# One TanH for four gates, one operation for the transform's spread, two f16 parts: an LSTM attention step on one core

## What is computed

```python
def step(carry, tgt):                     # tgt: one row of layernorm(x), 512 wide
    s, c, alpha = carry                   # 64, 64, 64 per batch row
    f = conv(alpha, conv_w)               # width 101
    e = einsum('a,bta->bt', va, tanh(enc_proj + (s @ Wa_s.T)[:, None, :] + f @ Wa_f + ba))
    alpha_new = softmax(where(mask, e, -1e30))
    g = einsum('bt,btd->bd', alpha_new, hbatch)
    y = tanh(g @ L_gy_w.T + L_gy_b + s @ L_sy.T) @ L_yy_w.T + L_yy_b
    rec = tgt @ L_ys.T + s @ L_ss.T + g @ L_gs_w.T + L_gs_b
    ig, fg, cg, og = split(rec, 4)        # 64 each
    c_next = sig(fg) * c + sig(ig) * tanh(cg)
    s_next = sig(og) * tanh(c_next)       # sig(z) = tanh(z / 2) / 2 + 1 / 2
```

## Time and profile before

| | us |
|---|---|
| median of three runs | 1523.16 |
| the three runs | 1520.36, 1523.16, 1537.06 |
| the profiled execution | 1518.94 |
| its span, first to last instruction | 1516.8 |

### The profile page before, as it was taken

The page is one execution under the profiler, slowest core; times in us unless marked ns, Lnnn a source line. Parts: engine busy times, 40 slices in busy tenths (PEclk is TensorE's granted clock), DMA queues, the critical chain, the costliest instruction groups (busy, mean ns, idle before and its releaser), DMA issues.

```text
span 1516.8 us, 43579 instructions
## 1 busy us (share of the span) xinstructions
PE 1395.5 (92%) x17408; PEld 919.4 (61%) x17408; DVE 943.9 (62%) x4478; ACT 544.3 (36%) x2143; POOL 275.1 (18%) x743
## 2 busy tenths in 40 slices
PE   4743887899999999999999999999999999999988
PEld 2533666466665676666666765556666666666546
DVE  4898455366665666675666657766655566566643
ACT  1343132134333344333334434443433333333321
POOL 3334222211111111111011111231110011111111
PEclk8565797999999999999999999999998999999989
DMA  8623000000000000000000001210000000000000
GB/s 278 240 90 90 0 1 4 1 2 2 3 2 2 2 2 2 3 2 2 2 2 2 2 19 45 58 37 2 2 16 2 2 2 9 9 2 3 9 9 14
DMA packets 19551, 37.06 MB, mean 24 GB/s; under 512 B 8436, under 2 KB 11683, under 8 KB 19348
## 3 DMA queue, kind: packets, MB, share of 16 engines
q1 hardware_dynamic: 19348, 34.28, 6.9%
HBM read 32.18 MB, written 2.10 MB: 23 GB/s over the span
## 4 chain that ended last, share of the span: by engine, by line
PE 83%; DVE 9%; issue 3%; ACT 2%; SPq 1%; POOL 1%; DMA 0%; DVEq 0%; ACTq 0%; POOLq 0%
PE bank L1921 9%; PE bank L1842 9%; PE bank L1635 9%; PE bank L1864 8%; PE bank L1652 6%; PE bank L1896 6%; PE bank L1673 4%; PE bank L1870 4%; PE bank L1618 3%; PE bank L1878 3%; PE bank L1905 3%; PE bank L1884 2%; PE bank L1612 2%; PE bank L1566 2%; PE bank L1518 2%
## 5 line engine op out<-in xcount | busy, mean ns | idle before, releaser
L1842 PE MATMUL bank<-ctx_lgs,identb 128*128 128x512 f16 (+2 forms) x685 | 190.9, 356 | 0.0
L1921 PE MATMUL bank<-ker_mem,uh 128*128 128x128 f32 x1020 | 184.3, 304 | 0.7 <-DVE ker_mem L1121 0.4
L1921 PEld LDWEIGHTS bank<-ker_mem,uh 128*128 128x128 f32 x1020 | 137.0, 194 | 66.1 <-DVE ker_mem L1121 48.9
L1635 PE MATMUL bank<-xT,wbig 128*128 128x256 f16 x1008 | 162.9, 275 | 0.0
L693 POOL TENSOR_TENSOR sscale<-ex,rinv 128x8 f32<-128x8 f32 x256 | 51.0, 199 | 506.8 <-DVE rinv L1106 506.8
L1439 ACT ACTIVATE xs<-gat 64x8 f32<-64x8 f32 x255 | 52.9, 207 | 244.2 <-DVE gat L1117 244.2
L1425 ACT ACTIVATE ker_mem<-bank 128x128 f16<-128x128 f32 x256 | 71.0, 278 | 184.8 <-PE bank L1864 184.8
L1430 ACT ACTIVATE eh<-bank,nmx 128x8 f16<-128x8 f32 x256 | 68.5, 268 | 172.4 <-PE bank L1887 172.4
L689 POOL COPY sscale<-s 64x4 f32<-64x4 f32 x256 | 59.0, 230 | 388.6 <-DVE s L1136 388.6
L1652 PE MATMUL bank<-wbig,interT 128*128 128x512 f16 x378 | 125.6, 399 | 0.0
L1121 DVE TENSOR_TENSOR ker_mem<-inv,ahn 128x128 f32<-128x128 f32 x510 | 124.0, 285 | 0.1
(11 more groups left out here) (238 smaller groups left out, 3290.9 us busy)
## 6 DMA issues: line engine op xcount, KB each, us to landing
wbig<-d_gate_qT SPq DMA_DIRECT2D x4, 896.0 KB, 9.9
wbig<-d_up_qT SPq DMA_DIRECT2D x4, 896.0 KB, 20.7
wbig<-d_down_qT SPq DMA_DIRECT2D x1, 3584.0 KB, 31.5
x_sb<-d_x SPq DMA_DIRECT2D x16, 128.0 KB, 6.0
d_out<-x_sb SPq DMA_DIRECT2D x16, 128.0 KB, 2.3
sscale<-d_gate_sT SPq DMA_DIRECT2D x2, 896.0 KB, 8.3
sscale<-d_up_sT SPq DMA_DIRECT2D x2, 896.0 KB, 4.3
work<-d_g1T SPq DMA_DIRECT2D x8, 224.0 KB, 2.5
```

What stands on the lines that cost most here:

```text
L1635: last = mm(tile_bank(n)[:, lo:lo + QC], w[wi][:, kt, it * P:(it + 1) * P], x_part[q % 2][xi][:, kt, :], start=(kt == 0 and wi + xi == 0), ...
L1842: mm(bank[7][:, 0:n], identb[:], hg2[:, 0].rearrange("p h g -> p (h g)")[:, 0:n], start=True, stop=True)
L1921: mm(bank[0][:, 0:P], uh[:, h, :], qv[:, h, :, :], start=False, stop=False, skip_group_check=True)
```

## The change

**Gate rows.** The permutation of the gate rows on the host is gone: `gat` holds input (partitions 0 to 63) and forget (64 to 127) in columns 0 to 3, cell and output in columns 4 to 7. ScalarE takes one TanH of 128x8 into `tg`. VectorE now needs two products of 64x4 (one of them reads partitions 0 to 63 and writes 64 to 127), since the cell state lies in a tile of its own, `cell`, on partitions 64 to 127. The scalings of weights and biases move with the rows.

**Spread.** The two operations of L1121 become one of 128x256 with one semaphore, `q_ready`. TensorE waits for it ahead of both f32 products. The wait on `kept` moves behind `sh`, ahead of the f32 state `s2`, which is what the copy reads.

**Parts.** `lss3` and `enc3` (three bf16 parts) become `lss2` and `enc2` (two f16 parts), the identity becomes f16 (`identh`). L1870 shrinks from ten matmuls to six, L1618 from three to two.

**Fill.** Half a unit moves from the place ahead of L1887 to the one ahead of L1878.

```diff
-                def spread(h):
-
-                    return nc.vector.tensor_tensor(qv[:, h, :, :], inv[:].unsqueeze(1).broadcast_to([P, B, TH]),
-                                                   ahn[:, 4 * h:4 * h + 4].unsqueeze(2).broadcast_to([P, B, TH]), ALU.mult)
-
                 dve.wait_ge(s["ahn_ready"], l + 1)
-                spread(0).then_inc(s["q0_ready"], 1)
+                nc.vector.tensor_tensor(qv.rearrange("p i b t -> p (i b) t"), inv[:].unsqueeze(1).broadcast_to([P, 2 * B, TH]),
+                                        ahn[:].unsqueeze(2).broadcast_to([P, 2 * B, TH]), ALU.mult).then_inc(s["q_ready"], 1)
+
+                dve.wait_ge(s["tg_ready"], l + 1)
+                nc.vector.scalar_tensor_tensor(ab[J:P, 0:4], tg[0:J, par, 0:4], 1.0, tg[0:J, par, 4:8], ALU.add, ALU.mult)
+                nc.vector.scalar_tensor_tensor(ab[J:P, 4:8], tg[J:P, par, 0:4], 1.0, cell[J:P, par, :], ALU.add, ALU.mult).then_inc(s["ab_ready"], 1)
+                dve.wait_ge(s["ab_ready"], l + 1)
+                nc.vector.scalar_tensor_tensor(cell[J:P, 1 - par, :], ab[J:P, 4:8], 0.5, ab[J:P, 0:4], ALU.mult, ALU.add).then_inc(s["c_ready"], 1)
+
+                dve.wait_ge(s["tc_ready"], l + 1)
+                nc.vector.scalar_tensor_tensor(sh[:], tg[J:P, par, 4:8], 1.0, tc_sb[J:P, :], ALU.add, ALU.mult).then_inc(s["sh_ready"], 1)
                 dve.wait_ge(s["kept"], l + 1)
-                spread(1).then_inc(s["q1_ready"], 1)
-
-                dve.wait_ge(s["tg_ready"], l + 1)
-                nc.vector.scalar_tensor_tensor(ab[:], tfi[:], 1.0, xs[:, par, 0:8], ALU.add, ALU.mult).then_inc(s["ab_ready"], 1)
-                dve.wait_ge(s["ab_ready"], l + 1)
-                nc.vector.scalar_tensor_tensor(xs[:, 1 - par, 0:4], ab[:, 0:4], 0.5, ab[:, 4:8], ALU.mult, ALU.add).then_inc(s["c_ready"], 1)
-
-                dve.wait_ge(s["tc_ready"], l + 1)
-                nc.vector.scalar_tensor_tensor(sh[:], xs[:, par, 8:12], 1.0, tc_sb[:], ALU.add, ALU.mult).then_inc(s["sh_ready"], 1)
-                nc.vector.scalar_tensor_tensor(s2[:, 1 - par, :], xs[:, par, 8:12], 1.0, tc_sb[:], ALU.add, ALU.mult).then_inc(s["s_ready"], 1)
+                nc.vector.scalar_tensor_tensor(s2[:, 1 - par, :], tg[J:P, par, 4:8], 1.0, tc_sb[J:P, :], ALU.add, ALU.mult).then_inc(s["s_ready"], 1)
@@
                 act.wait_ge(s["g_ready"], l + 1)
-                nc.scalar.activation(xs[:, par, 4:12], gat[J:P, :], ACT.Tanh, scale=0.5)
-                nc.scalar.activation(tfi[:], gat[0:J, :], ACT.Tanh, scale=0.5).then_inc(s["tg_ready"], 1)
+                nc.scalar.activation(tg[:, par, :], gat[:], ACT.Tanh, scale=0.5).then_inc(s["tg_ready"], 1)
                 act.wait_ge(s["c_ready"], l + 1)
-                nc.scalar.activation(tc_sb[:], xs[:, 1 - par, 0:4], ACT.Tanh, scale=0.5).then_inc(s["tc_ready"], 1)
+                nc.scalar.activation(tc_sb[J:P, :], cell[J:P, 1 - par, :], ACT.Tanh, scale=0.5).then_inc(s["tc_ready"], 1)
@@
-                for j in range(3):
-                    mm(bank[0][:, 0:P], identb[:], enc3[:, j, :], start=(j == 0), stop=False, skip_group_check=True)
+                for j in range(2):
+                    mm(bank[0][:, 0:P], identh[:], enc2[:, j, :], start=(j == 0), stop=False, skip_group_check=True)
@@
                 for gp in range(2):
-                    for j, st in ((0, sh), (1, sh), (2, sh), (0, sl), (1, sl)):
-                        last = mm(bank[2][:, 4 * gp:4 * gp + 4], lss3[:, j, gp * P:(gp + 1) * P], st[:],
-                                  start=(gp == 0 and j == 0 and st is sh), stop=(j == 1 and st is sl), skip_group_check=True)
+                    for j, st in ((0, sh), (1, sh), (0, sl)):
+                        last = mm(bank[2][:, 4 * gp:4 * gp + 4], lss2[:, j, gp * P:(gp + 1) * P], st[:],
+                                  start=(gp == 0 and j == 0 and st is sh), stop=(st is sl), skip_group_check=True)
                 last.then_inc(s["sp_done"], 1)
 
-                fill(UNIT, main_first, 384)
+                fill(UNIT + HALF_UNIT, main_first, 384)
                 pe.wait_ge(s["th_s"], l + 1)
@@
-                fill(UNIT, main_first)
+                fill(HALF_UNIT, main_first)
                 pe.wait_ge(s["th_lo_ready"], l + 1)
@@
                 fill(2 * UNIT, side_first)
+                pe.wait_ge(s["q_ready"], l + 1)
                 for h in range(2):
-                    pe.wait_ge(s[f"q{h}_ready"], l + 1)
                     mm(bank[0][:, 0:P], uh[:, h, :], qv[:, h, :, :], start=False, stop=False, skip_group_check=True)
                 fill(UNIT + HALF_UNIT, side_first)
@@
             dve.wait_ge(s["scale_ready"], 1)
-            in_parts(lss3[:], lssT[:])
+            in_halves(lss2[:], lssT[:])
@@
             dve.wait_ge(s["setup_cp"], 1)
-            in_parts(enc3[:], enc[:])
+            in_halves(enc2[:], enc[:])
```

More of the change, by code:

```diff
@@ L76, in shape_constants @@
         "c_time2": np.stack([np.tile(np.arange(TH), B), np.tile(np.arange(TH, T), B)]).astype(f32),
-        "c_gatescale": np.stack([np.where(np.arange(P) < J, 1.0, 2.0), np.ones(P)], 1).astype(f32),
+        "c_gatescale": np.stack([np.ones(P), np.where(np.arange(P) < J, 2.0, 1.0)], 1).astype(f32),
         "c_batchsel": (bm[None] == four).astype(f32),
@@ L137, in build @@
         enc = sb("enc", [P, P])
[L138 removed]
+        enc2 = sb("enc2", [P, 2, P], F16)
         hg = sb("hg", [P, 2, 256])
@@ L166, in build @@
         sl = sb("sl", [J, B], F16)
-        tfi = sb("tfi", [J, 8])
-        xs = sb("xs", [J, 2, 12])
-        ab = sb("ab", [J, 8])
-        tc_sb = sb("tc_sb", [J, B])
+        tg = sb("tg", [P, 2, 8])
+        cell = sb("cell", [P, 2, B])
+        ab = sb("ab", [P, 8])
+        tc_sb = sb("tc_sb", [P, B])
         s2 = sb("s2", [J, 2, B])
@@ L849, in in_halves @@
                 nc.vector.tensor_tensor(dst[:, 1], src, dst[:, 0], ALU.subtract).then_inc(s["part_ready"], 1)
-            def in_parts(dst, src):
-                for j in range(2):
-                    link(nc.vector.tensor_copy(dst[:, j], src))
-                    link(nc.vector.tensor_tensor(src, src, dst[:, j], ALU.subtract))
-                nc.vector.tensor_copy(dst[:, 2], src).then_inc(s["part_ready"], 1)
             moments(10, 2)
@@ L1840, in keep_busy @@
             def keep_busy(n):
-                mm(bank[7][:, 0:n], identb[:], hg2[:, 0].rearrange("p h g -> p (h g)")[:, 0:n], start=True, stop=True)
+                mm(bank[7][:, 0:n], identh[:], hg2[:, 0].rearrange("p h g -> p (h g)")[:, 0:n], start=True, stop=True)
             credit = [0]
@@ L1984 @@
     ctx = i["ctx_1024"]
-    perm = np.concatenate([np.arange(q * J, (q + 1) * J) for q in (1, 2, 0, 3)])
     kT = ctx.reshape(B, T, 8, HD).transpose(2, 3, 0, 1)
```

25 lines of the change are left out of this document (12 added, 13 removed).

## The result

The changed kernel is slower by 1%: 1542.41 us, the median of 20 runs (1531.14 to 1552.36), against 1524.52 for the kernel before (1516.54 to 1538.56, 20 runs). The ratio on record is 1.0098, with a 95% interval of 1.0070 to 1.0127; the two medians by themselves are 17.9 us apart, 1.2%. The forecast was 1489.5, in a range of 1474 to 1508.

A forecast was written before the change was run, and what follows sets the result against it. The prediction took the recurrence's step to bound the kernel (255 steps, 4.56 us each, three quarters of the span). Gains by kind of step summed to 31 us, 1518.9 to 1488, so a median of 1489.5, range 1474 to 1508.

The forecast's parts named there:

- The gates: Gate TanH and products: one TanH lets the product start 0.22 us earlier, two products start 0.08 apart, net 0.14.
- a tie: VectorE is free for the gate product at about 553.48, when TanH ends too; costs at most 0.02 us.
- The fill: Filler moved ahead of L1878: L1887 starts with `th_lo`, 0.07 us won; the maximum is next in line by 0.05.
- O: Origin of a step's times, the start of the matmul with `sl`; down-product steps' exponential was put at O + 1.38.
- The parts: L1870 loses four of ten matmuls, 0.10 us ahead of the filler; L1618's lost matmul and the setup's savings win nothing.
- The spread: One operation of 128x256 on VectorE takes 0.42 us, so L1921 starts 0.13 later than it did, less 0.07.
- TensorE decides: At the step's end TensorE's path comes last, so `sh` 0.21 us earlier wins the step only 0.16.
- rival 1: TensorE is not late and `sl` sets O: another 0.05 us in some 240 steps, 1477 us; chance 0.12.
- Rival 3: Waiting for the whole spread lengthens TensorE's path at L1921; at 0.57 for the spread, 1526 us; chance 0.04.
- rival 4: TensorE's clock falls: half-clocked steps cost about 0.85 us more, 36 more give about 1520 us; chance 0.06.
- Rival 2: The spread costs what the pair cost, 0.49 us: each step loses 0.07 of its 0.16, 1506 us; chance 0.10.
- rival 5: The one TanH's gain is partly hidden: at 0.27 us `sh` comes 0.06 later, O 0.01; inside the forecast's range.

The follow-up runs named there:

- experiment 5: Changed kernel with the first gate product written to partitions 0 to 63, where it reads, and the input gate's part of the cell left out: 1518.62 us.
- experiment 8: Changed kernel with the first gate product written to PSUM and the filler back at one unit each: 1498.53 us, ratio 0.9801 to the kernel before.
- experiment 14: Changed kernel, moved fill kept, with only the first gate product written to PSUM: 1524.85 us, ratio 0.9994 to the kernel before.
- experiment 4: Changed kernel with the two gate products in the other order: 1534.46 us.
- experiment 6: Kernel before with only the gates changed (rows reordered, one TanH, two products; wait for `kept` behind `sh`): 1568.93 us, ratio 1.0265.
- experiment 1: Changed kernel with the filler's sizes put back at one unit each: 1521.32 us, ratio 0.9969.
- experiment 2: Kernel before with only the fill moved (1.5 units ahead of L1878, 0.5 ahead of L1887): median 1567.69 us, ratio 1.0275.
- experiment 3: Kernel before with only the parts changed, two f16 in place of three bf16: 1513.79 us, ratio 0.9898.
- experiment 11: Kernel before with one spread for two and the wait for `kept` moved behind the state's first half, ahead of `s2`: 1531.30 us.
- experiment 7: Kernel before with only one spread for two, the wait for `kept` directly ahead of L1130's wait for `tg_ready`: 1538.72 us.
- experiment 9: Kernel before with a superfluous wait for `kept` written ahead of the wait for `tg_ready` at L1130: 1558.27 us.
- experiment 10: Kernel before with the superfluous wait for `kept` written behind the wait for `tg_ready`: 1534.13 us.
- experiment 12: Changed kernel with ScalarE's two waits ahead of the exponential swapped, `mx_ready` first and `et_done` second: 1543.50 us.
- experiment 13: Changed kernel with the filler's sizes of before, the first product in PSUM and ScalarE's two waits swapped: 1524.72 us, ratio 0.9984.

## Why the prediction was wrong

**The gates: this step failed.** "There are two products now; independent neighbours such as L1135 and L1136 start 0.08 apart, so the net is 0.14", and on other partitions "I take nothing, and bound it at one more 0.08". One TanH did bring its 0.22: it ends 0.41 behind the start of `gat`, where the second of two ended 0.63 behind. The hold took back 0.09 ahead of the first product, where the prediction had "a tie" that "costs at most 0.02": it let the product start before the spread's end. And the second product costs 0.17, not 0.08. So a net gain of 0.14 became a loss of 0.04. I had taken the price of a shift of partitions from ScalarE's L1439, which pays none. And I took the two operations of L1135 and L1136, which read and write the same partitions, for a measure of two that don't. Their counterparts in the changed kernel, L1123 and L1125, both read partitions 64 to 127 and start 0.08 apart: it is the change of partitions that costs, not where they lie. The 0.09 of the first product was taken away by experiments 5, 8 and 14. That of the second rests on the comparison with this pair, since no run had the second product on the partitions of the first; in every run it starts 0.014 behind the first one's end. The Trainium skill ("VectorE: DVE Perf Modes", Two Vector instructions with no wait between them) states the rule: an operation whose input or output starts in another quadrant of 32 partitions than the last read or write in the same memory starts only when all earlier ones are through. The traces agree in 253 of 255 steps each: the product starts 0.03 behind the spread's end when it writes partition 64 in SBUF (the changed kernel, experiments 4 and 6), and about 0.06 before that end when it reads and writes partition 0 (experiment 5) or writes partition 64 in PSUM (experiments 8 and 14). I had not weighed it.

**The fill: right about L1887, wrong about what is next in line.** "L1887 becomes free of filler": so it did. "The maximum ends at 551.63, and is used at 551.68; it is next in line by 0.05 us" failed: it is next in line at its end plus 0.10, since its wait is written second. So of the 0.07 to be won 0.01 was (1837 to 1824 from `sh`; from O it is 0.03, since `sl`'s matmul itself comes 0.01 later, at 482 for 470, and does so with the gates alone too, at 481). In the down-product steps the direction was as written, the exponential waits for the maximum, but it came at 1945 where "O + 1.38" is 1862: 0.02 of this is L1866, at O + 0.84 and not O + 0.82, and 0.06 is the longer delay behind the maximum. These 0.08 and the 0.18 of the gates, less the 0.05 by which TensorE was to limit the gain, turned the 0.07 won into 0.14 lost. Experiments 1 and 2 show the fill's share alone.

**The parts: right in the number, credited to the wrong edit.** The 0.10 ahead of the filler is there (L1878 at O + 0.61 in experiment 3, before O + 0.71), but I spent it on the moved filler. Alone it makes L1887 start with `th_lo` (experiment 3, -0.057 in the typical step), so that the fill's own gain, by the time it was applied, was zero.

**The spread: right.** 0.42, as taken, and its wait by itself costs nothing (experiment 11).

**TensorE decides: not reached.** With `sh` as it came, the load follows by 0.21, the sign that the prediction had named for rival 1, but because `sh` was not sooner. Where `sh` comes sooner it begins to show: the load follows by 0.27 in experiment 8 and by 0.29 in experiment 5, and from the start of the spread to the load it is then 1.44, where the forecast had 1.45. `sl`'s matmul is still on time there (480), so that TensorE decided no step length; whether it would have at the `sh` of the forecast, 0.13 sooner than in experiment 8, no run shows. Rival 3 named the side that came, but not the place: it put the price on TensorE behind the spread, and it lay on VectorE and in the waits.

**The clock (rival 4).** Steps above 4.8 us are 20 against 18 in the profiled executions. The runs say the same: at a mean granted clock of 0.926 or 0.927 five runs of the changed kernel took 1538.9 to 1546.8 us, and eleven of the kernel before 1523.3 to 1528.9, which is the whole difference. The clock had no part in the result. Rival 2 and rival 5 had none either.

In sum, in the typical step: the forecast had `sh` 0.21 sooner, limited by TensorE to 0.16. The two products on other partitions took 0.18 of the 0.21, the exponential's wait for the maximum 0.035 (4.519 for the 4.484 of experiment 1), `sl`'s later matmul 0.01, and some 0.01 is what L1887 had to give less than the 0.07 taken for it. That makes the 0.03 of loss that was measured.

## What to carry to other kernels

Before an operation is split or put on other partitions, look at what stands ahead of it on VectorE: an operation that starts on other partitions than its neighbour loses the overlap of both sides, here 0.09 us each, together nearly the 0.22 that the saved TanH took. Where an instruction has two waits, write first the one whose signal comes last; and count a moved filler not against the wait it frees but against the next in line with its own delay. Of edits that serve one gap (here fewer matmuls ahead of it, and filler taken out of it), price each with the other already in.

## What the runs showed of the hardware

The order of two waits on one instruction is worth 0.06 to 0.07 us. If the signal that comes last is the one written first, the instruction follows it by 0.03 to 0.04; if it is written second, by 0.10. Seen on VectorE (experiments 7, 9, 10, 11) and on ScalarE (2, 12, 13), with the other signal in time or long there. The traces show where it lies: of two waits ahead of an instruction, the one written second is an instruction of its own, an EVENT_SEMAPHORE of the engine's sequencer (0.02 us), which starts 0.03 to 0.04 behind its signal; the engine's instruction starts 0.063 (ScalarE) or 0.066 (VectorE) behind its start. So it stands between the signal and the work only if its signal comes last. Why the second and not the first is split off, no run shows.

The memory counts in the hold: an output in PSUM at partition 64 is not held behind an output in SBUF at partition 0 (product at 3600, 0.03 behind its signal, experiments 8 and 14).

Left open: the two kernels with the most steps above 4.8 us (43 in experiment 6, 38 in experiment 9, elsewhere 12 to 27) are among those with the longest steps, but experiment 2, as long, had 21. It is the granted clock that fell more often: its mean lies below 0.9 in 36 and 34 of their 254 steps, against 11 before, 8 after the change and 13 in experiment 2. In experiment 6 this is not one execution's luck, since all four runs have a mean clock of 0.909 to 0.914 over the kernel, against 0.910 to 0.934 in the seven runs of before beside them. Why it fell more often in these two kernels wasn't tried.
